# Q and K pieces split behind the probabilities, weights dequantised by GpSimd

## The reference

```
x = x + layernorm(attention(layernorm(x)))
x = x + layernorm(ffn(layernorm(x)))

attention: q = h @ Wq (32 heads of 128), k, v = h @ Wk, h @ Wv (8 groups)
           W = (codes - 8) * scales      # 4-bit codes as int32, a scale per 128 rows
           q, k = rope(q), rope(k)
           p = softmax(q k^T / sqrt(128) + causal mask);  out = (p v) @ Wo
ffn:       down(silu(gate(h)) * up(h)), 1376 wide, int8-like weights
```

## Time and profile before

| | before |
|---|---|
| median of 3 runs | 1536.74 us |
| profiled execution, its own time | 1538.01 us |
| its span | 1536.2 us |
| TensorE busy | 1431.4 us, 93% |
| VectorE busy | 1105.0 us, 72% |
| ScalarE busy | 987.4 us, 64% |
| GpSimd busy | 919.0 us, 60% |
| mean granted clock of TensorE | 0.979 |
| DMAs on SP's queue | 70.8% of 16 engines' span |

### The profile page before, as it was taken

One profiled execution on the slowest core, in us unless ns is written; L12 is line 12 of the kernel. 1 busy time (PEld: TensorE's weight loads), 2 busy tenths in 40 slices (PEclk: granted clock), 3 DMA queues, 4 the chain that ended last, 5 costly groups with the idle time before them and its releaser, 6 DMA issues.

```text
span 1536.2 us, 40725 instructions
## 1 busy us (share of the span) xinstructions
PE 1431.4 (93%) x11104; PEld 852.4 (55%) x11104; DVE 1105.0 (72%) x2500; ACT 987.4 (64%) x2582; POOL 919.0 (60%) x642
## 2 busy tenths in 40 slices
PE   4779799999999999999999999999999976999998
PEld 2445466556656665656656555665666553554543
DVE  7846477677768777777777777777777786776754
ACT  2576577777768777777777777777777763332321
POOL 2566577777767776777777777777777751010100
PEclk8999899999999999999999999999999988999999
DMA  8279989888888988998899989988988864011000
GB/s 269 63 161 176 170 166 163 165 160 168 165 159 165 164 161 155 173 161 169 158 165 171 172 159 167 171 169 154 167 164 163 150 117 95 15 48 42 15 28 28
DMA packets 522615, 217.15 MB, mean 141 GB/s; under 512 B 478944, under 2 KB 480704, under 8 KB 522432
## 3 DMA queue, kind: packets, MB, share of 16 engines
q1 hardware_dynamic: 519968, 210.53, 70.8%
q0 software_dynamic: 2464, 4.23, 1.6%
HBM read 55.32 MB, written 4.19 MB: 39 GB/s over the span
## 4 chain that ended last, share of the span: by engine, by line
PE 46%; POOL 12%; DMA 11%; issue 10%; SPq 10%; ACT 9%; DVE 1%; POOLq 0%; ACTq 0%; DVEq 0%
POOL p_lo L504 6%; DMA ot<-o_parts 5%; DMA swap<-other 4%; SPq L384 4%; PE ps_s L1027 4%; PE ps_s L1028 4%; POOL rot L488 4%; PE ps_p L792 4%; PE ps_p L793 4%; PE ps_p L794 4%; PE ps_p L816 3%; PE ps_p L817 3%; ACT p_hi L637 3%; PE ps_p L1041 2%; PE ps_p L1042 2%
## 5 line engine op out<-in xcount | busy, mean ns | idle before, releaser
L1118 DVE SCALAR_TENSOR_TENSOR y<-ps_p,wo_scale,y 128x512 f32<-128x512 f32 x512 | 381.0, 745 | 84.7 <-PE ps_p L817 70.8
L504 POOL TENSOR_TENSOR p_lo<-prob,p_hi 128x1280 f16<-128x1280 f32 x128 | 343.3, 2682 | 164.3 <-ACT p_hi L637 157.6
L628 ACT ACTIVATE prob<-prob,exp_bias 128x512 f32<-128x512 f32 (+3 forms) x512 | 285.6, 558 | 12.4
L1131 DVE CUSTOM_DVE_ANT_0 prob<-ps_s,mask 128x512 f32<-128x512 f32 (+3 forms) x512 | 236.8, 482 | 35.5 <-PE ps_s L831 30.2
L792 PE MATMUL ps_p<-x_hi,w_hi 128*128 128x512 f16 x640 | 244.9, 383 | 2.9 <-DVE w_lo L1052 1.5
L816 PE MATMUL ps_p<-ot,wo 128*128 128x512 f16 x512 | 199.4, 389 | 51.5 <-DMA ot<-o_parts 46.0
L793 PE MATMUL ps_p<-x_lo,w_hi 128*128 128x512 f16 x640 | 244.7, 382 | 0.0
L794 PE MATMUL ps_p<-x_hi,w_lo 128*128 128x512 f16 x640 | 244.3, 382 | 0.0
L488 POOL TENSOR_TENSOR rot<-rot,swap 128x512 f32<-128x512 f32 x160 | 203.2, 1278 | 51.3 <-DMA swap<-other 51.3
L845 PE MATMUL ps_o<-v_hi,ffn_w 128*128 128x128 f16 x1280 | 222.4, 220 | 10.1 <-DVE rot L1106 3.9
L846 PE MATMUL ps_o<-v_lo,ffn_w 128*128 128x128 f16 x1280 | 222.3, 220 | 0.0
(11 more groups left out here) (100 smaller groups left out, 2949.3 us busy)
## 6 DMA issues: line engine op xcount, KB each, us to landing
swap<-other SPq DMA_DIRECT2D x320, 128.0 KB, 3.1
w_code<-w_codes SPq DMA_DIRECT2D x36, 384.0 KB, 3.7
w_scale<-w_scales SPq DMA_DIRECT2D x36, 384.0 KB, 5.0
o_code<-o_codes SPq DMA_DIRECT2D x35, 256.0 KB, 2.9
swap<-x SPq DMA_DIRECT2D x16, 256.0 KB, 2.8
out<-z SPq DMA_DIRECT2D x16, 256.0 KB, 2.0
ffn_w<-x SPq DMA_DIRECT2D x3, 1024.0 KB, 9.8
ffn_w<-p_hi SPq DMA_TRANSPOSE x128, 3.6
```

The lines of the kernel that those rows point to most:

```text
L504: pool.tensor_tensor(p_lo[:, :], prob[:, hp, :], p_hi[:, :], ALU.subtract).then_inc(p_lod, 1)
L628: act.activation(prob[:, hp, a:a + w], prob[:, hp, a:a + w], ACT.Exp, bias=exp_bias[:, hp, i:i + 1], scale=-1.0, accum_out=exp_sum[:, hp, ...
L1118: dve.scalar_tensor_tensor(tile, ps_p[:, bank, :], scale, tile, ALU.mult, ALU.add).then_inc(o_add, 1)
L1131: dve.tensor_tensor_reduce(prob[:, hp, P_AT[i]:P_AT[i] + w], ps_s[:, bank, col:col + w], mask[:, S - w:], -SCORE_SCALE, NO_MINIMUM, ALU.ad ...
```

## The change

In every unit K and Q0 are projected in slot 0 and Q1 alone in slot 1. On ScalarE all exponentials and the probabilities' high half come before the pieces' high halves. On GpSimd `rope_low` of a piece moves one slot further back, ahead of `o_low`, and `rope_add` comes last; Q3 uses buffer 2. SP loads the output codes in slot 0 and the weights in slot 3. The dequantisation of the loop leaves VectorE; GpSimd does it in slot 1 with two instructions, (code - 8) * 1024 in place over the codes and then the product with the scales, so that `w_high` and `w_low` no longer scale by 1024 in the loop.

```diff
--- before.py
+++ after.py
@@ -68,7 +68,7 @@
 
 
 
-FULL = (("K",), ("Q0", "Q1"), ("Q2", "V"), ("Q3",))
+FULL = (("K", "Q0"), ("Q1",), ("Q2", "V"), ("Q3",))
 LAST = (("Y0",), ("Y1",), ("Y2", "X0"), ("Y3", "X1"))
 START = ("K", "Q0", "Q1", "Q2", "V", "Q3")
 ROPED = tuple(piece for piece in START if piece != "V")
@@ -120,12 +120,18 @@
     return made(U, r, h - 1, slots) if h else made(U - 1, 1 - r, HG - 1, FULL)
 
 
+def made_two_before(U, r, h, slots):
+
+
+    return made(U, r, h - 2, slots) if h > 1 else made(U - 1, 1 - r, HG - 2 + h, FULL)
+
+
 def rope_index(V, piece):
 
     return len(ROPED) * V + ROPED.index(piece)
 
 
-ROPE_BUF = {"K": 0, "Q0": 1, "Q1": 2, "Q2": 0, "Q3": 1}
+ROPE_BUF = {"K": 0, "Q0": 1, "Q1": 2, "Q2": 0, "Q3": 2}
 BUF_USERS = {buf: tuple(piece for piece in ROPED if ROPE_BUF[piece] == buf) for buf in range(3)}
 
 
@@ -268,6 +274,7 @@
         xt_hi = sem("xt_hi")
         xt_lo = sem("xt_lo")
         w_prod = sem("w_prod")
+        w_centred = sem("w_centred")
         w_hid = sem("w_hid")
         w_lod = sem("w_lod")
         o_cent = sem("o_cent")
@@ -436,9 +443,9 @@
                         turn_o(n - 2, h % 2)
                     if first:
                         load_o(h + 1)
-                    elif h == 1 and not last:
+                    elif h == 0 and not last:
                         load_o(U + HG)
-                    if h == 1 and more:
+                    if h == 3 and more:
                         load_w(U + 6, r)
                     if last:
                         if h == 0:
@@ -510,6 +517,16 @@
                 pool.wait_ge(oq_hid, n + 1)
                 pool.sem_inc(pool_passed)
                 pool.tensor_tensor(o_lo, o_f[:, :], o_hi, ALU.subtract).then_inc(oq_lod, 1)
+
+            def dequant(n, buf):
+
+                pool.wait_ge(w_in[buf], 32 * ((n >> 1) + 1))
+                pool.sem_inc(pool_passed)
+                centred = w_code[:, buf, :].bitcast(F32)
+                pool.tensor_scalar(centred, w_code[:, buf, :], -8.0, W_UP, ALU.add, ALU.mult).then_inc(w_centred, 1)
+                pool.wait_ge(w_centred, n - KT)
+                pool.sem_inc(pool_passed)
+                pool.tensor_tensor(w_product(n), centred, w_scale[:, buf, :], ALU.mult).then_inc(w_prod, 1)
 
             def start_rope(piece):
                 rope_add(0, 0, piece, START.index(piece) + 1)
@@ -539,17 +556,22 @@
                 for h in range(HG):
                     n = U * HG + h
                     p_low(n, h % 2)
-                    if not (first and h < 2):
+                    if first and h < 2:
+                        if h == 1:
+                            rope_low(0, 0, "Q3")
+                    else:
+                        for V, vpar, piece, bank, taken in made_two_before(U, r, h, slots):
+                            if piece != "V":
+                                rope_low(V, vpar, piece)
                         o_low(n - 2)
                     if first and h == 0:
                         start_rope("Q3")
-                        rope_low(0, 0, "Q3")
                     else:
-                        roped = [x for x in made_before(U, r, h, slots) if x[2] != "V"]
-                        for V, vpar, piece, bank, taken in roped:
-                            rope_add(V, vpar, piece, taken)
-                        for V, vpar, piece, bank, taken in roped:
-                            rope_low(V, vpar, piece)
+                        for V, vpar, piece, bank, taken in made_before(U, r, h, slots):
+                            if piece != "V":
+                                rope_add(V, vpar, piece, taken)
+                    if h == 1 and not last:
+                        dequant(U + 5, 1 - r)
                     if last and h:
                         power(2 * h - 1)
                     if last:
@@ -579,10 +601,10 @@
 
         @block.scalar
         def _(act):
-            def w_high(n):
+            def w_high(n, up=1.0):
                 act.wait_ge(w_prod, n + 1)
                 act.activation(flat(w_hi[:, bass.ds(n & (2 * KT - 1), 1), :]), w_product(n), ACT.Copy,
-                               scale=W_UP).then_inc(w_hid, 1)
+                               scale=up).then_inc(w_hid, 1)
 
             def o_centre(m):
 
@@ -659,10 +681,10 @@
                 act.activation(x_hi[:, :, t * P:(t + 1) * P], bank.rearrange("p (k c) -> p k c", k=KT),
                                ACT.Copy, scale=X_UP).then_inc(m_xhi, 1)
 
-            w_high(0)
+            w_high(0, W_UP)
             xt_high(0)
             for n in range(1, KT):
-                w_high(n)
+                w_high(n, W_UP)
             xt_high(1)
             rope_high(0, 0, "K")
             xt_high(2)
@@ -675,7 +697,7 @@
             rope_high(0, 0, "Q1")
             xt_high(3)
             rope_high(0, 0, "Q2")
-            w_high(4)
+            w_high(4, W_UP)
             for g in range(NG):
                 exps(0, 0, g)
             p_high(0, 0)
@@ -704,15 +726,14 @@
                     if more:
                         exps(n + 1, (h + 1) % 2, 0)
                         exps(n + 1, (h + 1) % 2, 1)
+                        exps(n + 1, (h + 1) % 2, 2)
+                        p_high(n + 1, (h + 1) % 2)
                     if first and h == 0:
                         rope_high(0, 0, "Q3")
                     else:
                         for V, vpar, piece, bank, taken in made_before(U, r, h, slots):
                             if piece != "V":
                                 rope_high(V, vpar, piece)
-                    if more:
-                        exps(n + 1, (h + 1) % 2, 2)
-                        p_high(n + 1, (h + 1) % 2)
                     for V, vpar, piece, bank, taken in made(U, r, h, slots):
                         if piece == "V":
                             v_high(V, vpar, bank, taken)
@@ -1046,10 +1067,10 @@
 
         @block.vector
         def _(dve):
-            def w_low(n):
+            def w_low(n, up=1.0):
                 dve.wait_ge(w_hid, n + 1)
                 at = bass.ds(n & (2 * KT - 1), 1)
-                dve.scalar_tensor_tensor(flat(w_lo[:, at, :]), w_product(n), W_UP, flat(w_hi[:, at, :]),
+                dve.scalar_tensor_tensor(flat(w_lo[:, at, :]), w_product(n), up, flat(w_hi[:, at, :]),
                                          ALU.mult, ALU.subtract).then_inc(w_lod, 1)
 
             def dequant(n, buf):
@@ -1140,13 +1161,13 @@
             dequant(0, 0)
             norm_rows(0)
             dequant(1, 1)
-            w_low(0)
+            w_low(0, W_UP)
             xt_low(0)
             dequant(2, 0)
-            w_low(1)
+            w_low(1, W_UP)
             dequant(3, 1)
-            w_low(2)
-            w_low(3)
+            w_low(2, W_UP)
+            w_low(3, W_UP)
             norm_stats(1)
             norm_rows(1)
             start_piece(0)
@@ -1162,7 +1183,7 @@
             norm_rows(3)
             dequant(4, 0)
             xt_low(3)
-            w_low(4)
+            w_low(4, W_UP)
             dve.wait_ge(mask_set, 1)
             for g in range(NG):
                 lows(0, 0, g)
@@ -1257,8 +1278,6 @@
                     for V, vpar, piece, bank, taken in made(U, r, h, slots):
                         if piece == "V":
                             take(V, vpar, piece, bank, taken)
-                    if h == 1 and not last:
-                        dequant(U + 5, 1 - r)
                     if h == 3 and not last:
                         w_low(U + 5)
                     if last and h:
```

## The result

Five runs of each kernel side by side: 1538.1 us before (1535.6 to 1543.7) and **1529.1 us** after (1524.7 to 1532.2), ratio 0.9936 [0.9918, 0.9955]. The changed kernel is 9 us faster where 21 were forecast; a second comparison of the same two kernels gave 0.9952 [0.9934, 0.997]. The profiled execution took 1532.2 us, its span 1530.4.

A forecast was written before the change was run, and what follows sets the result against it. TensorE was taken as the bound, only its pauses winnable: 27 us won, 9 given back, 3 at the start, so 21 off 1538.0 is 1517, median 1.3 lower: 1516 us. Forecast 1504 to 1524 (0.60), full range 1504 to 1543.

The forecast's parts named there:

- What bounds it, and how much is open: Steady window: TensorE is the bound; pauses cost 1.20 us per unit, 0.89 open to the change, 27 us in all.
- The new order: K and Q0 in slot 0, rounding behind probabilities: p_hi starts at 7.1 us, the tightest slot pair gains 2.7 us.
- The price of the dequantisation: GpSimd in slot 1: tensor_scalar 1.1, product 1.74, wait 0.1; 2.9 us together (2.4 to 5.3).
- Rivals A and B: GpSimd's dequantisation takes 3.6 us, total about 1531 (chance 0.20); or 4.5 us, total about 1555 (chance 0.13).
- With 2.9 us it just fits: Slot 2's `o_parts` transpose lands at 12.6, slot 3's first tile comes at 12.62; loss put at 0.2 us per unit.
- Slot 1's transpose "at 5.3, lands 8.5, needed 9.9": Output's transpose in slot 1: issued 5.3 us into the slot, landed at 8.5, before its need at 9.9.
- Rival D: Moving work between port-sharing engines gives nothing; only w_lo remains exposed, at most 2 us a unit, hidden; no separate chance.
- VectorE "busy 60 us less": Profile after the change: VectorE, having lost the dequantisation, is busy 60 us less.
- The start, 3 us: Start of the kernel: Q0 made a slot earlier shortens a 4.1 us wait for q_lo; 3 us gained (-4 to +6).
- The loads, 0.1 us per unit: Weights loaded in slot 3 and output codes in slot 0: 0.1 us lost per unit.
- The tail: Last unit and feed-forward: same instructions in nearly the same order, change 0 (within 2 us).

The follow-up runs named there:

- e8: Kernel before with only the new order and rounding, dequantisation on VectorE and loads in slot 1 as before: 1523.6 us, ratio 0.9916.
- e6: Changed kernel with w_lo early in slot 3 and GpSimd's tensor_scalar moved from slot 1 to slot 0: 1515.0 us, ratio 0.9867.
- e1: Changed kernel with w_lo moved behind the last y addition of slot 3: 1522.5 us, ratio to before 0.9905.
- e14: e8 with w_lo early in slot 3, as in e1: 1522.8 us, ratio to before 0.9899.
- e15: Changed kernel with both loads back in slot 1: 1525.9 us, ratio to before 0.9923.
- e7: Changed kernel with the dequantisation back on VectorE in slot 1, loads in their new slots: 1537.1 us, ratio to before 1.0003.
- e17: Changed kernel itself measured once more, beside its variants: 1528.7 us, ratio to before 0.9952.

## Why the prediction was right in direction and wrong in size

- *What bounds it, and how much is open.* Right. Pauses before were 35.0 us in 27 units by direct count, 1.30 a unit for a forecast of 1.20; outside the loop's turn 25.7, 0.95 for 0.89. A unit without a pause lasts 35.76 us after, for 35.84.
- *The new order.* Right in its mechanism: slots 0 and 1 lost all pauses before their output tiles, p_hi starts 7.2 to 7.6 us into slots 1 to 3 (7.1 forecast; 9.0 in slot 0, behind w_lo), and order alone (e8) is 13 us faster.
- *The price of the dequantisation.* Right, 2.84 us for 2.9; with it slot 2's p_lo starts at 3.02 (2.9) and its `o_parts` transpose at 9.09 (9.4). Rivals A and B, which needed 3.6 and 4.5 us, fall. That A's time, 1531, lies nearest to the measured 1529.1 is luck.
- *"With 2.9 us it just fits", 0.2 us per unit.* Mis-sized: with that and 0.1 for the loads 0.3 x 27 = 8 us should have been left, and it is 19.2. Slot 3's part is 6.8 us (0.25 a unit), close to the 0.2 itself, but e6 shows that the same work can be had for 0.02.
- *Slot 1's transpose "at 5.3, lands 8.5, needed 9.9".* **This step failed most.** Both of its terms were too small. It goes out at 6.06, because SP passes p_hi's transpose only behind the attention (2.07) and behind two swaps; the prediction took the time from GpSimd's chain and did not write down SP's for the slot to which it moved a second swap. And it lands in 4.50 us in 15 of 27 slots and in 3.12 in the others, for 3.2, the median of rows 8, whose own longest is 5.6. The 15 go out at 5.70 and land at 10.2 on the mean, 0.3 us too late; of the 1.4 us of slack the issue took 0.4 and the landing 1.3. The price is 10.2 us of pauses, where it had 0. Why the 15 land slowly stays open; an instruction packet is near each of them.
- *Rival D, "at most 2 us a unit and hidden".* The size was right (2612 - 952 = 1.66 us) and "hidden" was wrong. VectorE's minima of slot 0 stand behind w_lo, and so does K's projection in every fourth unit; e1 gives back 4.4 us in the 29 units, 5 to 7 by the ratios, and e14 against e8 2.6 by the ratios. The prediction used the rule of the shared port on the instruction that the change removes and took 952 ns for the one that stays, though the order that it praised moves p_lo onto it.
- *VectorE "busy 60 us less".* 5 us less, most of it from the same cause.
- *The start, 3 us.* Not found: -2.1 and +2.5 us in two executions.
- *The loads, 0.1 us per unit.* In the full change within 3 us of nothing (e15); in e7 13 us, which no step foresaw.
- *The tail.* Right: unchanged.
- The two moves of e6, w_lo early in slot 3 and the tensor_scalar in slot 0, bring 1515.0 us. That this is the forecast's number is partly luck: slot 2's 10.2 us of pauses are still in it, and unit 2's slot 2 begins 6 us earlier than before in its trace, where the forecast had 3.

## What to carry to other kernels

When an order makes one engine earlier, list what VectorE and GpSimd run against each other at that new time, the instructions that stay included; w_lo went from 0.95 us to 2.6 without being touched. For every transfer that a chain relies on, write the issuing queue's own order down, with the wait at its head, in the slot as it will be. Take the time to land from its spread and not from its median: here half of slot 1's transposes took 4.5 us where the median said 3.2. New work goes where its engine waits anyway: here the same 0.84 us cost 7.5 us in one slot and nothing in another.

## What the runs showed that I had not expected

- The dequantisation alone and the order alone bring 5 and 13 us, and the change with both 9; in the 29 units it is 8.3, 8.3 and 8.4.
- In every trace the transposes of `o_parts` in slot 1 land in 3.1 to 3.4 us on the mean, or in 4.1 to 4.7 where a packet of the instruction queue is near.
- The place of loads that nothing waits for changes the time by 13 us with VectorE's dequantisation (e7, e8) and by 3 at most with GpSimd's (e15, e17), through "issue" waits of VectorE after the loop's turn.
- The turn of the loop costs TensorE 7.7 to 12.8 us in 27 units in every version. It is the largest pause left in the best one; its cause is open, and so is why it grew when the outputs were taken later.
